# A perceiver block on one core: early context kept in the values' buffer, and value products in two batches of four groups per head

## What is computed

```python
def _L0_xattn_ref(query, key_value, Wq, bq, Wk, bk, Wv, bv, Wo, bo):
    q = (query @ Wq + bq).reshape(B, Nq, H, D).transpose(0, 2, 1, 3)      # B 4, Nq 256, H 16, D 16
    k = (key_value @ Wk + bk).reshape(B, Nkv, H, D).transpose(0, 2, 1, 3)  # Nkv 4096
    v = (key_value @ Wv + bv).reshape(B, Nkv, H, D).transpose(0, 2, 1, 3)
    attn = jnp.clip(jnp.einsum('bhqd,bhkd->bhqk', q, k) * scale, -CLAMP, CLAMP)
    attn = jax.nn.softmax(attn, axis=-1)
    return jnp.einsum('bhqk,bhkd->bqhd', attn, v).reshape(B, Nq, Cq) @ Wo + bo

x = x + _L0_xattn_ref(_layernorm(x), ctx_768, ...)
x = x + _L0_attn_ref(_layernorm(x), ...)      # causal self-attention
x = x + _L0_ffn_ref(_layernorm(x), ...)       # slot routing, top 8 of 64 slots
```

## The kernel before

| step | filler |
|---|---|
| 0 | lower bound of the clip, one matmul (L1250) |
| 1, 5, 9, 13 | value products, two groups each (L1217); at 1 it is groups 6 and 7 of the head before |
| 3, 7 | one half each of a k projection for chunk i + 20 (heads 0 to 43) |
| 4 | `finish`: sums of the head before (L1226) |
| 11 | shift rows of the next head (L1149) |
| 11, 15 | one half each of a v projection for chunk i + 17 (heads 0 to 46) |

## Time and profile before

### The profile page before, as it was taken

How to read it: one execution, slowest core, us unless ns; L and a number is a source line. 1 busy time by engine, 2 the same in 40 slices (tenths; PEclk the granted TensorE clock), 3 DMA queues, 4 the chain that set the end, 5 groups by cost and what they waited for, 6 DMA issues and landing times.

```text
span 1380.5 us, 33263 instructions
## 1 busy us (share of the span) xinstructions
PE 1289.3 (93%) x10494; PEld 764.5 (55%) x10494; DVE 979.6 (71%) x2160; ACT 716.0 (52%) x1299; POOL 175.4 (13%) x226
## 2 busy tenths in 40 slices
PE   6888999999999999999999999999999887896987
PEld 4665665666666656666666655444444464455534
DVE  5526887888888888888888888888888458634222
ACT  1213666666666666666666666666666613241111
POOL 3503111111111111111111110000000140000000
PEclk9989999999999999999999999999999999998665
DMA  6874445544445544445444443345422000000000
GB/s 168 258 153 118 96 96 122 114 101 101 100 105 109 106 101 95 106 109 108 100 97 106 108 98 57 62 91 142 73 49 50 2 1 1 1 2 1 1 0 30
DMA packets 110612, 115.23 MB, mean 83 GB/s; under 512 B 17462, under 2 KB 102267, under 8 KB 104317
## 3 DMA queue, kind: packets, MB, share of 16 engines
q1 hardware_dynamic: 101510, 105.89, 35.2%
q10 hardware_dynamic: 8960, 7.87, 2.1%
HBM read 84.79 MB, written 28.84 MB: 82 GB/s over the span
## 4 chain that ended last, share of the span: by engine, by line
PE 79%; DVE 11%; issue 3%; ACT 3%; DMA 2%; SPq 1%; POOL 1%; ACTq 0%; DVEq 0%; POOLq 0%
PE acc L1217 17%; PE st L1243 15%; PE mx L1132 15%; PE kps L1123 6%; PE kps L1114 6%; DVE mxp L786 5%; PE misc L1226 2%; ACT prob L670 2%; PE st L1123 2%; DVE amax L951 1%; PE st L1104 1%; PE acc L1114 1%; PE setB L1402 1%; DMA qst<-qscr 1%; PE setB L1396 1%
## 5 line engine op out<-in xcount | busy, mean ns | idle before, releaser
L786 DVE TENSOR_REDUCE mxp<-mx 128x1 f32<-128x512 f32 x1024 | 682.8, 686 | 191.4 <-PE mx L1132 180.6
L601 ACT ACTIVATE prob<-st 128x512 f32<-128x512 f32 x1024 | 570.8, 597 | 350.2 <-PE st L1243 343.3
L1132 PE MATMUL mx<-kst,qst 96*128 96x512 bf16 x1024 | 392.0, 383 | 21.0 <-DVE mxp L786 9.0
L1243 PE MATMUL st<-qst,kst 99*128 99x256 bf16 x2048 | 392.4, 273 | 1.6 <-ACT prob L601 1.5
L1243 PEld LDWEIGHTS st<-qst,kst 99*128 99x128 bf16 x2048 | 178.3, 100 | 202.8 <-issue 84.7
L1217 PE MATMUL acc<-prob,vh 128*32 128x256 f32 x4096 | 275.1, 386 | 3.5 <-POOL vh L464 3.0
L1217 PEld LDWEIGHTS acc<-prob,vh 128*32 128x32 f32 x4096 | 106.9, 109 | 124.5 <-issue 70.5
L1132 PEld LDWEIGHTS mx<-kst,qst 96*128 96x128 bf16 x1024 | 98.9, 97 | 64.4 <-DVE mxp L786 38.8
L1114 PE MATMUL kps<-ctx,wk 128*128 128x256 f32 (+1 forms) x432 | 114.3, 390 | 16.3 <-DMA wv<-in_L_xattn_bv 12.8
L1123 PE MATMUL kps<-wv,ctx 128*128 128x256 f32 (+1 forms) x376 | 101.6, 392 | 0.0
L464 POOL COPY vh<-v_sb 128x512 f32 (+1 forms) x64 | 39.0, 610 | 490.9 <-PE acc L1217 490.9
(11 more groups left out here) (355 smaller groups left out, 1035.0 us busy)
## 6 DMA issues: line engine op xcount, KB each, us to landing
kst<-kscr SPq DMA_DIRECT2D x64, 384.0 KB, 4.7
kst<-kscr SPq DMA_DIRECT2D x192, 128.0 KB, 5.1
kscr<-kparts SPq DMA_DIRECT2D x108, 192.0 KB, 2.5
ctx<-in_ctxT SPq DMA_DIRECT2D x87, 128.0 KB, 2.0
ctx<-in_ctxT SPq DMA_DIRECT2D x87, 64.0 KB, 2.2
ctx<-in_ctxT ACTq DMA_DIRECT2D x40, 128.0 KB, 2.6
kscr<-o_sb SPq DMA_DIRECT2D x20, 192.0 KB, 3.0
qst<-qscr SPq DMA_DIRECT2D x192, 8.0 KB, 4.4
```

What stands on the lines that cost most here:

```text
L601: act.activation(prob[:, s % 8, :], st[bank_of[s]][:, :], ACT.Exp).then_inc(exp_done, 1)
L786: dve.reduce_max(mxp[:, par, s // 8, s % 8:s % 8 + 1], mxb[s % 2][:, :], AX.X).then_inc(max_red, 1)
L1132: pe.matmul(mxb[s % 2][:, :], qst[0:96, slot, qt * P:(qt + 1) * P], kst[0:96, slot, n * 512:(n + 1) * 512], start=True, stop=True).then_in ...
L1243: mm = pe.matmul(st[bank_of[s]][:, n * T:(n + 1) * T], kst[0:99, u, (2 * s + n) * P:(2 * s + n + 1) * P], qst[0:99, u, :], start=True, sto ...
```

## The change

1. **Early context.** Chunks 0 to 15 are loaded once, into the places of `v_sb` that their own values will take; chunks 16 to 19 go to `ctx4`. SP issues all of these loads and no longer ACT: chunks 0 to 3 among the weights, 4 to 15 right after them, ahead of the first write of k. Chunks 20 and 21 are loaded by SP behind the writes of chunks 16 to 19.
2. **q parts.** The first part of q is written once and read with a broadcast, 2 DMAs in place of 6.
3. **Value products.** Exponentials have 16 places (`prob`, and the buffers `xn` and `xnT`, idle in this stage). Groups 0 to 3 run at step 9, groups 4 to 7 at step 1 of the next head.
4. **Fillers.** The second half of k stands at step 6, that of v at step 14.
5. **Copies.** `save_acc` and the shift rows' copy go from DVE to ACT. DVE takes k's rest a step earlier.
6. **GpSimd.** The first `vh` copy stands ahead of the bias additions. The clip, which does not run with this data, is written out over 16 tiles.

```diff
+        def exps(s):
+            return prob[:, s, :] if s < 8 else xn_p[:, s - 8, :] if s < 12 else xnT_p[:, s - 12, :]
+        early_slot = {16: 0, 17: 3, 18: 2, 19: 1}
+        def early_ctx(c):
+            return v_sb[:, 2 * c:2 * c + 2, :] if c < 16 else ctx4[:, early_slot[c], :, :]
...
         @block.sync
+            def load_early(c):
+                n = c % 4 if c < 16 else early_slot[c]
+                sp.dma_start(early_ctx(c)[:, 0, :], a["ctxT"][c, 0:P, :]).then_inc(ctx_in[n], 16)
+                sp.dma_start(early_ctx(c)[0:C2, 1, :], a["ctxT"][c, P:C, :]).then_inc(ctx_in[n], 16)
...
+            load_early(3)
+            for c in range(4, 16):
+                sp.wait_ge(ctx_in[c % 4], 32 * (c // 4))
+                load_early(c)
...
             for g in range(2):
-                for r in range(3):
-                    sp.dma_start(qscr1[g * P:(g + 1) * P, r, :], q1[:, g, :]).then_inc(qscr_w, 16)
+                sp.dma_start(qscr1[g * P:(g + 1) * P, :], q1[:, g, :]).then_inc(qscr_w, 16)
...
             for c in range(16, KLEAD):
                 write_early(c)
+            sp.wait_ge(v_ps, VLEAD)
+            load_ctx(0, KLEAD)
+            sp.wait_ge(k_ps, KLEAD)
+            load_ctx(1, KLEAD + 1)
...
         @block.gpsimd
-            pool.wait_ge(bo_in, 32)
-            add_bias(0)
             pool.wait_ge(v_out, VLEAD)
             pool.wait_ge(rest_set, 16)
             copy_vh(0, 0, 0, 0)
+            pool.wait_ge(bo_in, 32)
+            add_bias(0)
...
         @block.scalar
                     if s % 2 == 0:
-                        wait(act, pv_done, i * 8 + s // 2 - 3)
-                    act.activation(prob[:, s % 8, :], st[bank_of[s]][:, :], ACT.Exp).then_inc(exp_done, 1)
+                        wait(act, pv_done, i * 8 + s // 2 - 7)
+                    act.activation(exps(s), st[bank_of[s]][:, :], ACT.Exp).then_inc(exp_done, 1)
...
+                    if s == 2 and not first:
+                        save_acc(i - 1)
+                    if s == 12 and near:
+                        shift_rows(i + 1, (u + 1) % 4)
...
         @block.vector
+            dve.memset(v_sb[C2:C2 + 1, 1:32:2, :], 1.0).then_inc(rows_set, 1)
...
-                    if s == 2 and not first:
-                        save_acc(i - 1)
-                    if s == 9 and k_job:
+                    if s == 8 and k_job:
                         k_rest(i + KLEAD, u % 2)
...
         @block.tensor
                     if s == 1 and not first:
-                        for g in (6, 7):
+                        for g in range(4, 8):
                             pv_group(i - 1, (u + 1) % 2, g)
-                    if s in (3, 7) and k_job:
+                    if s in (3, 6) and k_job:
...
-                    if s in (11, 15) and v_job:
+                    if s in (11, 14) and v_job:
...
-                    if s in (5, 9, 13):
-                        if s == 5:
-                            wait(pe, vh_ready, i + 1)
-                            wait(pe, acc_out, i)
-                        for g in range(2):
-                            pv_group(i, u % 2, (s - 5) // 2 + g)
+                    if s == 9:
+                        wait(pe, vh_ready, i + 1)
+                        wait(pe, acc_out, i)
+                        for g in range(4):
+                            pv_group(i, u % 2, g)
```

More of the change, by code:

```diff
@@ L311, in load_stacks @@
                 cols = bass.ds(b * T, T)
[L312 removed]
+                sp.dma_start(qst[0:48, slot, :], qscr1[rows, cols].unsqueeze(1).to_broadcast([DH, 3, T])).then_inc(done, 16)
                 for n, scr in enumerate((qscr2, qscr2, qscr3)):
@@ L321, in write_early @@
                                  early_parts(c)[:, g, :, :]).then_inc((kscr_w, spare_w)[c % 4 // 2][c % 2], 16)
-            for c in range(6):
+            for c in range(4):
+                write_early(c)
+            for c in range(16, KLEAD):
+                sp.wait_ge(ctx_in[early_slot[c]], 32 * 4)
+                load_early(c)
+            for c in range(4, 6):
                 write_early(c)
@@ L570, in early_first @@
                                ACT.Copy).then_inc(k_1, 1)
-            for c in range(4):
-                load_early(c, c)
             act.wait_ge(consts, 11)
@@ L612, in _ @@
             for u in range(4):
-                head(0, u, True, u > 0)
+                head(0, u, True, u > 0, True, u == 0)
             with act.Fori(1, 11, 1) as it:
                 for u in range(4):
-                    head(it, u, True, True)
+                    head(it, u, True, True, True, False)
             for u in range(4):
-                head(11, u, False, True)
-            with act.Fori(12, 16, 1) as it:
+                head(11, u, False, True, True, False)
+            with act.Fori(12, 15, 1) as it:
                 for u in range(4):
-                    head(it, u, False, False)
+                    head(it, u, False, False, True, False)
+            for u in range(4):
+                head(15, u, False, False, u < 3, False)
+            save_acc(NH - 1)
             act.wait_ge(head_out, NH)
@@ L816, in shift_step @@
                                       apply_absolute_value=True).then_inc(flag_abs, 1)
-            SHIFT_AT = {LEAD + n: n for n in range(6)} | {12: 6, 13: 7}
+            SHIFT_AT = {LEAD + n: n for n in range(6)} | {13: 7}
             def max_step(it, u, s, near, far):
@@ L883, in _ @@
                 head(15, u, False, u < 3, u < 2)
-            save_acc(NH - 1)
             take_sums(NH - 1)
@@ L1108, in normed, with project_k @@
                 return xn[:, t, c * P:(c + 1) * P]
-            def project_k(bank, slot, g):
+            def project_k(bank, chunk, g):
                 for n in range(2):
@@ L1114, in project_k, with project_v @@
                     mm = pe.matmul(bank[:, g * CH:(g + 1) * CH], wk[0:rows, n, g * P:(g + 1) * P],
-                                   ctx4[0:rows, slot, n, :], start=(n == 0), stop=(n == 1))
+                                   chunk[0:rows, n, :], start=(n == 0), stop=(n == 1))
                 if g == 1:
                     mm.then_inc(k_ps, 1)
-            def project_v(bank, slot, t):
+            def project_v(bank, chunk, t):
                 for n in range(2):
                     rows = P if n == 0 else C2 + 1
-                    mm = pe.matmul(bank[:, t * D:(t + 1) * D], ctx4[0:rows, slot, n, t * P:(t + 1) * P],
+                    mm = pe.matmul(bank[:, t * D:(t + 1) * D], chunk[0:rows, n, t * P:(t + 1) * P],
                                    wv[0:rows, n, :], start=(n == 0), stop=(n == 1))
@@ L1224, in finish @@
                 wait(pe, acc_out, i + 1)
+                wait(pe, head_out, i)
                 for qt in range(QT):
```

98 lines of the change are left out of this document (48 added, 50 removed).

## The result

| | before | after |
|---|---|---|
| median, beside each other | 1374.2 (1370.1 to 1379.2, 6 runs) | 1389.5 (1386.2 to 1395.6, 6 runs) |
| ratio | | 1.0105, 95% interval 1.0076 to 1.0135 |
| span of the profiled execution | 1380.5 | 1393.0 |
| head 0's bound matmul | 121.48 | 112.83 |
| head 0 (to head 1's bound matmul) | 22.12 | 22.96 |

The change made the kernel 1% slower: 1387 was forecast, 1389.5 measured. The difference of the two spans, 12.6, is the sum of the lines: -8.7 + 0.8 + 12.5 + 0.1 + 5.2 + 0.9 + 1.8.

A forecast was written before the change was run, and what follows sets the result against it. TensorE without a gap bounds heads 0 to 43, waits for reductions the late heads, DMAs the start. Start -7.5, head 0 +0.5, projecting heads +13.2, late +3, last +2.5 sum to +11.7 on 1375.4: 1387, range 1372 to 1397.

The forecast's parts named there:

- The `mx` loop: Projecting heads: maxima after two steps without filler wait for their bank, at steps 9, 14 and 1; +0.76 us per head.
- Merged batches: Every projecting head: two value batches in place of four save two ways in and out, 0.46 us per head.
- Rival B: The bank loop does not bite in projecting heads, each 0.46 shorter; 1342, or 1359 with half the waits; chance 0.06.
- The start: K and V stage up to the first maxima: fewer q copies, no second context reading; -7.5 us, bounds -1 to -14.
- up to 6 of the gain: Start: 24 context issues ahead of k's first write eat up to 6 us if places for parts don't cover it.
- the memset: Start: the extra memset on DVE runs while x is on its way, cost nothing; about 1 if x comes first.
- Head 0: First head: a 3.7 us wait for chunk 20's context replaces 3.03 for `vh`; +0.5 us, bounds -3 to +3.
- Rival C: The start gives more, waits shrink and TensorE's clock stays up: 1376, results from 1368 to 1380; chance 0.19.
- Late heads: Heads projecting only v or nothing: VectorE idles longer at two batches, less two copies; +3 us, bounds -2 to +8.
- Last heads: Heads 62 and 63: ACT sets the pace, idles longer at long batches and gets `save_acc`; +2.5 us, bounds 0 to 4.
- The copies on ScalarE: `save_acc` and shift rows moved to ACT are covered; at most 0.5 us a head if cover is missing.
- Rival D: SP, carrying all loads, bounds the start; k's writes slip and the -7.5 is lost: 1394.5 or 1399; chance 0.13.

The follow-up runs named there:

- One bare pair: Kernel before the change, with only the second half of k's projection moved from step 7 to step 6: 1391.4 us, ratio 1.0118.
- the quarters kernel: Changed kernel with each half projection cut in two, at steps 3, 5, 6, 7 and 11, 13, 14, 15: 1349.8 us, ratio 0.9801.
- Context first: Changed kernel with chunk 20's context load issued behind the write of chunk 17, not of chunk 19: 1381.4 us, ratio 1.0042.
- the one with everything and the long clip: Changed kernel with half projections cut in two, four value batches in late heads and chunk 20's context loaded behind chunk 17's write: 1377.3 us, ratio 1.0003.
- the short-clip one: The quarters kernel with GpSimd's passed-over clip as three groups of large tiles, 12 instructions for 64: 1350.2 us, ratio 0.9810.

## Why the prediction was right, and where it was not

**The `mx` loop: right.** Forecast 0.29, 0.29 and 0.18 at steps 9, 14 and 1; measured 0.28, 0.29 and 0.18. One bare pair alone gave +0.30 a head, all taken away -0.78. **Merged batches: right.** 0.46 forecast, 0.48 by the quarters kernel, a batch of 1.97 for 1.95. Net +0.30 over 43 heads is 12.9, against 12.5 between the two profiles (the kernel before had one head of 16.5). Rival B is refuted: the loop bites wherever a pair is bare, in projecting heads too.

**The start: about right up to head 0, by other steps.** -7.5 was forecast at head 0's bound matmul. The profile of before gives -8.7, but 2.7 to 4.1 of that belong to the longer low clock of that one execution; against the two others of the old start it is -4.6 and -6.0. The K stage's wait and its low clock did go, and the stack took 9.1 for 11.0, as said. But the first write of k slid from 20.1 to 26.9 behind the 24 context issues (13.7 of SyncE's queue, for a forecast of 18), eight more for chunks 16 to 19, which the text did not count, stand between the fourth write and the fifth, and the last write moved up by only 2, not 6: this is the case that the text priced at "up to 6 of the gain" and chose against. PE also waits anew near the beginning, so that its transposes start at 24.8 to 26.5 in all kernels with the new start, and at 22.7 to 23.2 in the three with the old one. LayerNorm starts at 10.96 there, when two memsets of 3.47 one after the other are through; with the old start it waits for x, until 9.39 to 10.95. So the memset costs up to 1.6 there, where the text had 0 to "about 1".

**Head 0: the mis-sized term.** +0.5 was forecast, bounds -3 to +3, and +0.84 measured, but that agreement is luck. The wait of 3.85 for context came where 3.7 was forecast. The 22.12 of before, though, holds a wait of 3.03 for `vh` and low clock behind it (0.85 granted over the head): the bare-pair kernel, which has the same start and in head 0 only the bare pair more, takes 19.45, waits 1.37 and is granted 0.91. With the same heads the new start makes head 0 longer by 4.4 (22.96 for 18.58, changed heads) and 4.2 (23.68 for 19.45, old heads, but for the bare pair). That eats most of the start's gain: head 1 begins at 135.3 to 137.0 in the five kernels with the new start and the old context order, and at 136.9 and 137.4 in the two others with the old start. Start and head 0 together give 1.6 in profiles with the same heads and 2.2 to 2.8 between medians, where the sum had 7.0. What was not seen is that the wait could be had away for nothing. Rival C priced that wait at 3, and 3 for the clock (its sum took 5 of the 6), and Context first measured 6.5.

**Late heads: right in size, wrong in kind.** +3 was forecast for two long idle times of VectorE; measured +5.2, of which 3.9 are head 52's (its wait of 2.16 for GpSimd and the low clock behind it), which the prediction did not have at all: it has no term for the written-out clip, code that does not run. Without it a head is 0.09 longer, for a forecast of 0.2. **Last heads: within the bounds.** +2.5 forecast; measured 0.9 in head 62 and 2.8 in head 63, whose last `finish` matmul comes 15.7 after its bound matmul and not 12.9. The code behind it happened to run 1.0 shorter.

**The copies on ScalarE: right**, hidden, at 0.38 each; that their removal from VectorE is worth 0.5 in a late head is argued, not shown by a run of its own.

In sum start and head 0 fell short by some 4 to 5 us, the late heads overran by 2 and the last ones by 1, and 1389.5 for 1387 is inside the range: the medians rose by 15.3 where 11.7 was forecast. These misses add up to more than that; the rest is within what medians of six runs leave open, so the closeness is in part luck. Rival D had the right kind of cost (SyncE's issues do hold the writes of k), but the larger part of the loss is head 0's wait for the load that stands behind those writes; rival C did not come.

## What to carry to other kernels

Where two buffers go round between a fast producer and a reducer, the spacing of the other work matters as much as its amount: for every use of a buffer count what stands since its last use but one, and cut long fillers until no gap is below the loop's time. Code that is passed over is not free on an engine whose signal others wait for, so keep branch bodies short and ask for such a signal late. A change that loses may hold a gain that its placing hides: the batches that came with a loss of 1% here are part of a kernel that gains 2.8%.

## What the runs showed that was not expected

A skipped body of 64 GpSimd instructions in the loop over heads makes the code behind it 4 to 8 us late in nine late heads, in the changed kernel as in the one with everything and the long clip; 12 instructions do not, and neither does the body of 32 in a loop of its own that the kernel before has. Which wait then meets the lateness decides between 4 us and 38.

From the last `finish` matmul of head 63 to the end the code is the same in all kernels here, and it takes 270.5 to 280.1 us, depending on the profile. The stretch from 240 to 280 us behind head 63's bound matmul, in the changed kernel (277.3) and in the short-clip one (270.5):

```profile
1340.02:1380.02 40.00, 34.37 (x87) 16.41 (x88) 8.19 (x23) 4.90 (x7) 0.00 (x0) 0.50 0.00 0
```

```profile
1300.58:1340.58 40.00, 34.66 (x114) 17.60 (x112) 9.64 (x24) 5.54 (x8) 0.00 (x0) 0.71 0.03 11
```

TensorE's clock is at 1.2 GHz all through in the one and partly back at 2.4 GHz in the other. The five profiles with two batches in the last heads took 270.5 to 277.3, and of the seven with four batches six took 278.1 to 280.1 and one 272.7; whether the heads before have a part in it or it is chance stays open. Single profiles can thus differ by up to 9.5 us beyond what a change does. If the runs without a profile vary alike, that is why the short clip's 5 us and the four batches' 7 did not show in four runs, and why the two halves of the change don't add up.
